# One-hot scatter steps: where TensorE and SyncE read their step addresses and gate values from

## The reference

```python
neigh = x[col]                                       # 200000 edges, 6250 nodes, 256 features
agg = jax.ops.segment_sum(neigh, row, num_segments=n)
deg = jax.ops.segment_sum(jnp.ones((row.shape[0],), x.dtype), row, num_segments=n)
h = (x + agg / deg) @ W.T + b                        # twice: two layers over the same edges
```

## Time and profile before

| | us |
|---|---|
| median of 3 runs | 3077.56 |
| lowest and highest | 3074.18, 3082.22 |
| span of the profiled execution | 3077.5 |
| edges sorted, mixer (0 to 591) | 591 |
| steps (591 to 1541) | 950 |
| two layers (1541 to 2765) | 1224 |
| experts (2765 to 3077) | 312 |

### The profile page before, as it was taken

One profiled execution on the slowest core, in us unless ns is written; L12 is line 12 of the kernel. 1 busy time (PEld: TensorE's weight loads), 2 busy tenths in 40 slices (PEclk: granted clock), 3 DMA queues, 4 the chain that ended last, 5 costly groups with the idle time before them and its releaser, 6 DMA issues. The chain is left out here.

```text
span 3077.5 us, 50865 instructions
## 1 busy us (share of the span) xinstructions
PE 2554.9 (83%) x14238; PEld 1578.3 (51%) x14238; DVE 1928.2 (63%) x4802; ACT 1418.0 (46%) x3757; POOL 170.6 (6%) x160
## 2 busy tenths in 40 slices
PE   0776556676778888889989999997999999967997
PEld 0334334333334444455578888884444444444665
DVE  8878899899899999999833222221233233346555
ACT  0786455266656666677822222222122222235666
POOL 0000000000000000000000000000111111114000
PEclk9988788798989999999999999999999999988999
DMA  5000000022134244234365444445444444401000
GB/s 171 19 18 13 13 12 13 16 85 84 73 117 162 106 160 157 98 129 163 113 222 174 146 148 149 142 150 175 152 139 138 137 137 138 138 11 38 26 22 30
DMA packets 167928, 318.02 MB, mean 103 GB/s; under 512 B 30228, under 2 KB 139541, under 8 KB 167765
## 3 DMA queue, kind: packets, MB, share of 16 engines
q1 hardware_dynamic: 115860, 230.55, 23.6%
q10 hardware_dynamic: 51776, 85.24, 7.6%
q0 software_dynamic: 128, 0.26, 0.0%
HBM read 203.09 MB, written 112.92 MB: 103 GB/s over the span
## 5 line engine op out<-in xcount | busy, mean ns | idle before, releaser
L1186 PE MATMUL banks<-outer,ring 128*128 128x512 f16 x2450 | 544.2, 381 | 16.7 <-DMA outer<-table,heavy 9.0
L817 ACT ACTIVATE ring<-banks 128x512 f16<-128x512 f32 (+1 forms) x637 | 366.8, 576 | 342.9 <-POOLq L668 339.0
L1183 PE MATMUL banks<-tabs,ring 128*128 128x257 f16 x2250 | 495.9, 273 | 4.8 <-DMA ring<-counts 4.8
L1184 PE MATMUL banks<-tabs,ring 128*128 128x256 f16 x2250 | 495.8, 272 | 0.0
L1186 PEld LDWEIGHTS banks<-outer,ring 128*128 128x128 f16 x2450 | 239.3, 98 | 302.6 <-issue 23.1
L818 ACT ACTIVATE banks<-banks 128x512 f32<-128x512 f32 (+1 forms) x637 | 368.3, 578 | 0.0
L1798 DVE TENSOR_SCALAR ring<-val,outer 128x512 f16<-128x512 f16 x1102 | 319.3, 357 | 41.1 <-PE banks L1149 40.3
L1149 PE MATMUL banks<-ring 128*128 128x512 f16 x920 | 270.7, 410 | 66.6 <-SPq L558 31.4
L961 PE MATMUL banks<-tabs,xT 128*128 128x512 f32 x400 | 205.2, 661 | 55.1 <-ACT xT L726 55.1
L1183 PEld LDWEIGHTS banks<-tabs,ring 128*128 128x128 f16 x2250 | 218.3, 97 | 34.7 <-issue 5.5
L1184 PEld LDWEIGHTS banks<-tabs,ring 128*128 128x128 f16 x2250 | 219.2, 97 | 26.4
(11 more groups left out here) (364 smaller groups left out, 3807.9 us busy)
## 6 DMA issues: line engine op xcount, KB each, us to landing
counts<-ring ACTq DMA_DIRECT2D x84, 896.0 KB, 3.9
ring<-counts SPq DMA_DIRECT2D x94, 800.0 KB, 4.7
ring<-counts SPq DMA_DIRECT2D x94, 768.0 KB, 4.1
outer<-in_fw SPq DMA_DIRECT2D x8, 1024.0 KB, 7.8
outer<-in_x SPq DMA_DIRECT2D x5, 1280.0 KB, 13.5
x_transposed<-xT SPq DMA_DIRECT2D x50, 128.0 KB, 1.7
outer<-in_x SPq DMA_DIRECT2D x25, 256.0 KB, 2.9
xT<-x_transposed SPq DMA_DIRECT2D x25, 256.0 KB, 2.7
```

What stands on the lines that cost most here:

```text
L817: act.activation(held[:, b, 0:q, c, :], cell_bank.rearrange("p (q r) -> p q r", r=P), ACT.Copy, scale=0.25).then_inc(s_cell, 1)
L1183: mm(o[:, 0:D + 1], a, xtab[l][:, cb, D:2 * D + 1], start=cb == 0, stop=False)
L1184: m = mm(o[:, 0:D], a, xtab[l][:, cb, 0:D], start=False, stop=cb == NT - 1)
L1186: m = mm(o, a, xtab[l][:, cb, 0:2 * D], start=cb == 0, stop=cb == NT - 1)
```

## The change

The packing goes. DVE writes, for each step, the bank's offset as it is used (0, 512, 1024 or 1536, `bank_at`), and, for each group, the cell that its gate waits for (`gates`). PE loads sixteen offsets in one call for every 16 steps and uses each as it is; SP loads eight gate values in one call for every 8 groups. `cell1` loses its second buffer, the eight constants on POOL go, and `CONSTS` falls with them.

```diff
-CONSTS = 14 + 8
+CONSTS = 14
@@
-def loaded(nc, ap, engine, most):
+def loaded(nc, ap, engine, most, least=1):
     return nc.values_load_multi_w_load_instructions(
-        ap, engines=(engine,), min_val=1, max_val=most,
+        ap, engines=(engine,), min_val=least, max_val=most,
@@
-        place = val[0:1, 784:792].bitcast(U16)
@@
-        cell1 = outer[0:1, 9664:10176].bitcast(U16).rearrange("p (b t) -> p b t", b=2)
+        bank_at = outer[0:1, 9664:10176].bitcast(U16).rearrange("p (b t) -> p b t", b=2)
         ends = outer[0:1, 10176:10496].bitcast(U16)
-        step_bank = outer[0:1, 12384:12640].bitcast(U16)
-        words = outer[0:1, 12640:12704].bitcast(U16).rearrange("p (b t) -> p b t", b=2)
+        cell1 = outer[0:1, 12384:12640].bitcast(U16)
+        gates = outer[0:1, 12640:12768].bitcast(U16).rearrange("p (b t) -> p b t", b=2)
@@ SP, per group
-                u = n * 4 + 3 - PB[q]
-                cell, = loaded(nc, cell1[:, q % 2, u:u + 1], mybir.EngineType.SP, G + 1)
-                sp.wait_ge(s_free, cell)
+                u = n - PB[q] // 4
+                if u % 8 == 0:
+                    cells = loaded(nc, gates[:, q % 2, u:u + min(8, NG - n)], mybir.EngineType.SP, G + 1)
+                sp.wait_ge(s_free, cells[u % 8])
                 sp.sem_inc(s_gate, 1)
@@ POOL, constants
-            for n in range(8):
-                pool.memset(place[:, n:n + 1], 4 ** n).then_inc(s_const, 1)
@@ PE
-            def banks_of_steps(at):
-
-                if at.shape[-1] == 2:
-                    at = at.bitcast(I32)
-                return nc.values_load_multi_w_load_instructions(
-                    at, engines=(mybir.EngineType.PE,), skip_runtime_bounds_check_because="used under masks of two bits alone")[1][0]
@@ PE, per group
                 if t0 % 16 == 0:
-                    u = (t0 - PB[q]) // 8
-                    word = banks_of_steps(words[:, q % 2, u:u + min(16, STEPS - t0) // 8])
+                    u = t0 - PB[q]
+                    at = loaded(nc, bank_at[:, q % 2, u:u + min(16, STEPS - t0)], mybir.EngineType.PE, (NBK - 1) * 512, 0)
                 pe.wait_ge(s_gate, n + 1)
                 pe.wait_ge(s_hot, n + 1)
                 for t in range(t0, t0 + 4):
-                    k, j = divmod(t % 16, 5)
-                    if j == 0 and k:
-                        word = word >> 10
-                    at = (word & (NBK - 1 << 2 * j)) * (512 >> 2 * j)
-                    mm(ps[:, bass.ds(at, 512)], hot_c[t // 8 % 3][:, :, t % 8], hot_r[t % RSLOTS],
+                    mm(ps[:, bass.ds(at[t % 16], 512)], hot_c[t // 8 % 3][:, :, t % 8], hot_r[t % RSLOTS],
                        start=False, stop=False, skip_group_check=True).then_inc(s_step, 1)
@@ DVE, piece_rows
-                ins = dve.scalar_tensor_tensor(cell1[:, q % 2, 0:n], iota16[0:1, 0:n], PB[q] + 1.0, bank[6][0:1, 0:n],
-                                         op0=ALU.add, op1=ALU.subtract)
-                link(ins)
-                link(dve.tensor_scalar(step_bank[:, 0:n], cell1[:, q % 2, 0:n], NBK - 1, None, op0=ALU.bitwise_and))
-                eights = step_bank[:, 0:n].rearrange("p (w k) -> p w k", k=8)
-                link(dve.tensor_tensor(eights, eights, place.unsqueeze(1).to_broadcast([1, n // 8, 8]), op=ALU.mult))
-                with nc.allow_low_precision(reason="whole numbers below 2 ** 16"):
-                    dve.tensor_reduce(words[:, q % 2, 0:n // 8], eights, axis=AX.X, op=ALU.add).then_inc(s_ready, 1)
+                link(dve.scalar_tensor_tensor(cell1[:, 0:n], iota16[0:1, 0:n], PB[q] + 1.0, bank[6][0:1, 0:n],
+                                              op0=ALU.add, op1=ALU.subtract))
+                dve.tensor_copy(gates[:, q % 2, 0:n // 4], cell1[:, 0:n].rearrange("p (g k) -> p g k", k=4)[:, :, 3])
+                dve.tensor_scalar(bank_at[:, q % 2, 0:n], cell1[:, 0:n], NBK - 1, 9, op0=ALU.bitwise_and,
+                                  op1=ALU.logical_shift_left).then_inc(s_ready, 1)
                 dve.wait_ge(s_ready, q + 1)
```

## The result

The changed kernel takes 3455.84 us, median of 4 runs (3450.68 to 3457.46), against 3079.89 us for the kernel before on the same chip: a ratio of 1.1229, 95% interval 1.1216 to 1.1242. It is slower, as forecast, but by 376 us where 97 were forecast, and far outside the range of 3105 to 3285.

The account below looks back on a forecast made before the run. DVE's one-hots were taken to bound the steps, PE close behind; PE's load would move the bound to a 7.0 us chain per block. Terms by stretch sum to +97 us: 3077.5 + 97 = 3175 us, range 3105 to 3285.

Parts of the forecast that it names:

- Where, and which way: In the steps, 591 to 1541 us: slower by 97 us, everything behind later by the same amount and otherwise unchanged.
- The price of a load: PE's load of sixteen offsets: 303 ns plus 15 x 243 ns, 3.95 us, in each of 138 loads.
- the pair row: SP's one load of two values in the trace, 497 ns: 243 ns for the second value.
- The overlap with `out_product`: Three stretches, 47.9 blocks: the tiles' matmuls run beside the load; a block goes from 6.78 to 7.15 us, +17.7 us.
- The chain: Per block of 16 steps: load, first matmuls, DVE's one-hots and four steps sent off make a cycle of 7.0 us.
- Half clock: Rival, chance 0.10: PE idles some 3 us a block and restarts at half clock; +0.9 us a block, 3230 to 3290 us.
- ACT, "Cost 0": ACT's cells in a mean block: 5.4 us of work, under the cycle of 7.0, so no cost.
- some tenths a block at the end: ACT's only risk: some tenths a block at the end, where cells are short.
- Masks "next to nothing": PE's 19 ALU_OPs per 16 steps: removal saves some 1.7 us of issue a block, alone next to nothing.
- SP: SP's 69 loads of eight gate values, 1.96 us each, hidden under PE's loads: cost 0.
- the bound of 117: SP's loads, if PE's load did not cover them: up to 69 x 1.7 = 117 us.
- The range: 3105 to 3285 us, holding the forecast, cheaper values, 303 ns a value and half of half clock: some 0.83.

Follow-up runs that it names:

- e_few_bytes: Changed kernel, with each of ACT's stores of the count matrix writing one cell of its seven, SP filling zeros before: 3364 us.
- the controls: Changed kernel with four added float32 matmuls of 8 columns before PE's load, instead of 320: 3495 against 3445 us; with one cell of seven stored, 3405 against 3330.
- e_tiny: Changed kernel, with four float32 matmuls of only 8 columns queued ahead of PE's load in blocks without pieces: 3495 us, ratio 1.1359.

## Why the prediction was wrong, point by point

- **Where, and which way**: right. All of the loss is in the steps; the rest is unchanged to a few us.
- **The price of a load**: the pair row gave 3.95 us, the quiet load is 3.78 (0.234 a value), so reading the price per value from one row of two values held. What failed is taking the quiet price for all 138. The forecast used 303 ns although showed single loads of up to 1452; in the mean of the same 138 loads it was 0.43 us. The mean of the sixteen is 4.54, which is 81 us over 138 loads; `e_few_bytes` took as much off the loads and 91 us off the kernel.
- **The overlap with `out_product`**: failed, and in the stretch with the most blocks. "Their matmuls queue up and run beside the load", +0.15 us a block; the tiles stand behind the load, on the chain, and a pair of blocks with tiles takes 2.4 to 2.9 us more than a bare one, where 0.3 was allowed: some 55 to 65 us over 25 pairs (from traces, not from an edit).
- **The chain**: right where its conditions hold (6.9 and 7.0 us at 725.9 and 732.8; 7.17 in the mean of the 13 blocks with quiet load and full clock; 8.3 us in the mean of the twelve blocks with pieces, for 8.2). They hold in few blocks.
- **Half clock**: named and priced at +0.9 us a block, but as a rival at 0.10, and the sum had nothing for it. It cost 50 to 74 us by the controls, for part of the way back to full clock. A hole of 3.2 us did not bring the clock down everywhere: it was 1.00 from 732.8 to 739.8 us, a block with the hole shown above. It is lowest where loads are long, but `e_few_bytes`, with a mean load of 3.95 us, had only 0.84 in the steps. What starts the fall is not shown.
- **ACT, "Cost 0"**: failed. 5.4 us of work in a cycle of 7.0 is a rate. After a hole what counts is the latency of the first cell of the burst, of which only "some tenths a block at the end" were allowed. Cutting ACT's work gave 29 to 34 us (16 of them in the kernel before as well), and 50 with the other two causes lessened.
- **Masks "next to nothing"**: true for the kernel before, where DVE sets the pace; in the changed one they would cost some 80 us. The sum's chain already sent off its four steps without them (0.5 us; 0.44 measured), so no term of it failed here.
- **SP**: right. No cost under PE's load, 12 us without that cover, far below the bound of 117.
- **The range**: each rival was priced alone, on top of a chain with the quiet load at full clock, though long loads, half clock, late gates and tiles lengthen the same cycle and add up. That is why it ended at 3285. The parts measured (91, 50 to 74, 29 to 50 and 55 to 65 us) and the forecast's 97 come to 320 to 380 of the 376 us; they were not measured independently, so the sum closes only roughly.

## What to carry to other kernels

PE's sequencer sends nothing while it loads registers, at 0.23 us a value here; register operations, some 0.09 us each, were the cheaper way to spread one loaded word over many uses. Where a chain of buffers sets a cycle, price a hole in it with everything that the hole does: the means of the rows rather than their medians, the clock that an idle PE gets back with, and the latency (not the rate) of each engine that frees a buffer. Other work fills the hole only if it stands in front of it in the queue, so look up where it stands. Effects that lengthen one cycle belong into one sum and not into separate rivals. And an edit that cures a cause by adding instructions needs the same instructions without the cure as its control; without `e_tiny` the clock would have passed for harmless.

## What the runs showed of the hardware

- A load of registers costs 0.05 us and 0.234 us for each value on PE (4, 8 and 16 values: 0.98, 1.92, 3.78 us), and SP's eight take 1.66 us. The Trainium skill (Runtime: NRT & Kernel Launch, Instruction fetch mechanics) gives about 200 ns per register even in bulk: the trace agrees in kind, and SP's 0.201 us a value (1.659 less 0.254, over 7) in size; PE's value costs more.
- It gets longer while DMAs move: 3.79 us with no packet, 4.91 with ACT's stores, 5.59 with SP's transfers as well; a single one from 0.30 to 0.71 us in the kernel before (35 loads beside ACT's stores).
- The granted clock of the steps was 0.82 with one hole in each block (3.24 us at the quiet load of 732.8, 4.88 at a load of 5.3), and 0.91 when matmuls filled some 2 us of it; `e_tiny`, with as many matmuls of 8 columns, had 0.83.
- PE's sequencer sends off four steps (first address to fourth) in 0.64 us at the least with a mask for each (0.75 in the mean, kernel before), and in 0.34 us without (0.44 in the mean, changed kernel).
